# An attention core regrouped: one 512-column context product for four heads, in place of one 65-column product for each head

## The reference, cut to what matters

```python
# L0 attention, 1024 tokens of 256 features; H, NOPE, ROPE, V_DIM, KV_RANK = 16, 128, 64, 128, 64
q = (hidden_states @ q_proj_w.T).reshape(b, s, H, Q_DIM).transpose(0, 2, 1, 3)
compressed = hidden_states @ kv_a_proj_w.T
k_pass_lat = compressed[..., :KV_RANK]
k_rot = compressed[..., KV_RANK:]
kv = _rmsnorm(k_pass_lat, kv_a_ln_w) @ kv_b_proj_w.T        # per head: k_pass (128), v (128)
scores = jnp.einsum('bhqd,bhkd->bhqk', q, k) * scaling      # causal
probs = jax.nn.softmax(scores.astype(jnp.float32), axis=-1).astype(q.dtype)
out = jnp.einsum('bhqk,bhkd->bhqd', probs, v)
return out.transpose(0, 2, 1, 3).reshape(b, s, H * V_DIM) @ o_proj_w.T
```

## Time and profile before

| | before |
|---|---|
| median of 3 runs | 997.33 us |
| runs | 988.61, 997.33, 999.35 us |
| span of the profiled execution, first to last instruction | 985.5 us |
| attention, first transposes of tile 1 to the last tile's residual | 84.2 to 472.3 us of the span |
| PE busy in that stretch | 374.84 of 388.10 us |
| PEld, DVE, ACT, POOL busy there | 329.48, 224.91, 185.27, 133.04 us |

### The profile page before, as it was taken

How to read it: one execution, slowest core, us unless ns; L and a number is a source line. 1 busy time by engine, 2 the same in 40 slices (tenths; PEclk the granted TensorE clock), 3 DMA queues, 4 the chain that set the end, 5 groups by cost and what they waited for, 6 DMA issues and landing times.

```text
span 985.5 us, 17100 instructions
## 1 busy us (share of the span) xinstructions
PE 850.1 (86%) x5125; PEld 700.9 (71%) x5126; DVE 452.2 (46%) x1231; ACT 322.4 (33%) x768; POOL 261.2 (27%) x432
## 2 busy tenths in 40 slices
PE   5999998999999999998279993476888799999964
PEld 4778886788999888887179992466866555556653
DVE  4123664647475665664334442466755122222244
ACT  1233554654554444443024341121232022222210
POOL 2003535242414132134300003777306000000241
PEclk9997999999999999998589997698989999999988
DMA  6339401010001000001569994556352111111111
GB/s 172 83 93 415 149 1 43 7 39 12 32 2 43 2 26 18 2 27 60 204 209 352 355 358 131 177 171 212 125 171 80 33 43 43 43 43 32 49 59 38
DMA packets 83856, 102.20 MB, mean 104 GB/s; under 512 B 16096, under 2 KB 74464, under 8 KB 82528
## 3 DMA queue, kind: packets, MB, share of 16 engines
q1 hardware_dynamic: 64112, 69.20, 21.7%
q0 software_dynamic: 7680, 20.98, 6.5%
q10 hardware_dynamic: 12016, 11.41, 3.4%
HBM read 67.22 MB, written 34.34 MB: 103 GB/s over the span
## 4 chain that ended last, share of the span: by engine, by line
PE 33%; POOL 7%; issue 5%; DVE 3%; DMA 2%; ACT 0%; POOLq 0%; SPq 0%; DVEq 0%; ACTq 0%
PE scores L1634 9%; POOL area L569 6%; PE scores L1484 5%; PE acc_ps L1654 4%; PE probsT_ps L1598 3%; PE scores L1495 2%; PE scores L1287 2%; PE probsT_ps L1473 1%; PE scores L1288 1%; PE scores L1289 1%; DMA area<-xe_d 1%; PE probsT_ps L1644 1%; POOL rstd L517 1%; POOL xe_d L525 1%; PE misc_ps L1619 1%
## 5 line engine op out<-in xcount | busy, mean ns | idle before, releaser
L1384 PE MATMUL misc_ps<-area 128*128 128x65 f32 x1152 | 152.5, 278 | 4.7 <-DVE ctx_n L903 1.6
L1384 PEld LDWEIGHTS misc_ps<-area 128*128 128x128 f32 x1152 | 146.5, 196 | 11.0 <-ACT area L649 2.5
L887 DVE TENSOR_REDUCE neg_max<-scores 128x1 f32<-128x128 f32 (+7 forms) x128 | 96.8, 756 | 67.6 <-PE scores L1358 64.8
L511 POOL TENSOR_TENSOR q_lo<-area,q_hi 128x128 fp32r<-128x128 f32 x128 | 59.1, 461 | 179.7 <-ACT q_hi L668 171.4
L649 ACT COPY area<-probsT_ps 128x512 f32<-128x512 f32 (+3 forms) x128 | 64.9, 507 | 120.0 <-PE probsT_ps L1368 115.4
L643 ACT ACTIVATE area<-scores,neg_max 128x128 f32<-128x128 f32 (+7 forms) x128 | 95.7, 747 | 0.0
L1368 PE MATMUL probsT_ps<-ident,area 128*128 128x128 f32 x576 | 91.0, 281 | 2.1 <-ACT ctxT L653 1.8
L1634 PE MATMUL scores<-area 128*128 x184 | 86.7, 615 | 4.0 <-issue 2.9
L1287 PE MATMUL scores<-kT_hi,q_hi 128*128 128x512 f32 (+3 forms) x192 | 77.3, 402 | 6.3 <-POOL q_lo L511 4.8
L1368 PEld LDWEIGHTS probsT_ps<-ident,area 128*128 128x128 f32 x576 | 69.1, 149 | 7.6 <-ACT ctxT L653 6.9
L569 POOL DMA_INDIRECT area<-ye_d,fetch_now x64 | 63.9, 999 | 23.5 <-issue 18.5
(11 more groups left out here) (217 smaller groups left out, 1496.4 us busy)
## 6 DMA issues: line engine op xcount, KB each, us to landing
area<-gate_up SPq DMA_DIRECT2D x32, 384.0 KB, 6.9
xe_d<-area SPq DMA_DIRECT2D x8, 1024.0 KB, 10.3
area<-w SPq DMA_DIRECT2D x8, 1024.0 KB
area<-xe_d SPq DMA_DIRECT2D x32, 256.0 KB, 7.0
ye_d<-area ACTq DMA_DIRECT2D x32, 256.0 KB, 5.9
area<-down SPq DMA_DIRECT2D x32, 192.0 KB, 7.1
area<-w SPq DMA_DIRECT2D x8, 512.0 KB, 7.9
area<-xd_d SPq DMA_DIRECT2D x23, 128.0 KB, 2.2
```

The source lines that it names most:

```text
L887: dve.tensor_reduce(neg_max[:, u:u + 1], banks[u][:, 0:(qt + 1) * P], AX.X, ALU.max, negate=True).then_inc(max_ready, 1)
L1384: last = pe.matmul(ctx_ps, probsT[:, u, k * P:(k + 1) * P], latent[:, k, :], start=k == 0, stop=k == qt)
```

## The change

Heads are taken in groups of four. A slot is one head's turn: group G, head i of four, `n = 4G + i`. In slot n the scores of head n + 2 are made, the steps of group G - 1 and the output of one head of group G - 2 (`output(4(G - 2) + i)`), so that three groups are under way at once. All loops over pairs are gone; every instruction of the attention stands in the program once.

- Transposes of one block of all four heads go to one bank (`transpose_probs(G, k)`), ScalarE copies the whole bank (`copy_hi`), and `context(G, k)` holds the 128x64 block of `latent` as weights and moves 512 columns of transposed probabilities. There are 144 such products, one for each group and block, in place of 576.
- The context comes out transposed (64 partitions by 4 x 128 columns); ScalarE copies it once for a group (`copy_ctx`), and the 64 transposes of the context go.
- The output is made for each head, with 64 partitions: 128 products of 256 columns in place of 64. They aren't accumulated in PSUM: VectorE multiplies each with the inverse row sum and adds it to x1 (`add_head`), and the next one waits for that (`out_read`), since they share one bank. Row sums come from the exponential's own accumulator.
- The read-outs of the router move to the second half of the outputs' bank (`acc`). `pe_slot` waits for `out_read` before each of the three steps, and for the step's read-out before the next output.
- GpSimd makes both halves of the query, for two heads at once and three pairs ahead; ScalarE's rounding goes. Sends are issued one in every second slot.
- Rows of probabilities of ten heads are kept, in a part of the memory for expert weights, so the first loads of expert weights wait for the last transposes. The zero rows become half as long. The `wvo` products have both halves of the partitions filled and are copied as 512 columns.

```diff
...
+QUAD = 4
+SETS = HEADS // QUAD
+GROUPS = TILES * SETS
+ROWS_KEPT = 10
...
+        wv_h = cutA3(2, 2, RANK)
...
+        wvo = cutA3(HEADS * HID)
...
+        latent = wq_h.rearrange("p a b -> p (a b)").rearrange("p (t r) -> p t r", t=TILES)
...
+        pT_sb = cutA3(2, BANK)
...
-        x1T_ps = pT[1][:, 0:HID]
...
+        out_ps = acc[:, 0:HID]
+        x1T_ps = acc[:, HID:2 * HID]
...
+        def steps_at(G, place):
+
+
+            if not 0 <= G < GROUPS:
+                return []
+            n = tile_of(G) + 1
+            return [k for k in range(n + 1) if k * 8 // (n + 1) == place]
+
...
+        def head_slots(body):
+
+            for G in range(GROUPS + 2):
+                for i in range(QUAD):
+                    body(G, i, QUAD * G + i)
...
+            sp.wait_ge(pT_ps, blocks_to(GROUPS))
...
+            def split_q(m):
+
+                qt, h = divmod(2 * m, HEADS)
+                two = qT[:, h * T:(h + 2) * T].rearrange("p (h t) -> p h t", h=2)[:, :, qt * P:(qt + 1) * P]
+                if m >= 3:
+                    pool.wait_ge(scores_ready, 2 * (m - 3) + 2)
+                pool.tensor_copy(q_his[m % 3], two).then_inc(q_half, 1)
+                pool.wait_ge(q_half, m + 1)
...
+            def copy_hi(b):
+                act.wait_ge(pT_ps, b + 1)
+                if b >= 2:
+                    act.wait_ge(ctx_step, b - 1)
+                act.copy(pT_sb[:, b % 2, :], pT[b % 2][:]).then_inc(hi_done, 1)
+
+            def copy_ctx(G):
+                act.wait_ge(ctx_step, blocks_to(G + 1))
+                if G >= 2:
+                    act.wait_ge(out_ready, QUAD * (G - 1))
+                act.copy(ctxT[0:RANK, G % 2, :], ctx_ps[0:RANK, :]).then_inc(ctx_copied, 1)
...
+            def act_slot(G, i, n):
+                for place in (2 * i, 2 * i + 1):
+                    for k in steps_at(G - 1, place):
+                        if k <= tile_of(G - 1):
+                            copy_hi(blocks_to(G - 1) + k)
+                if i == QUAD - 1 and 0 <= G - 1 < GROUPS:
+                    copy_ctx(G - 1)
+                if n + 2 < TILES * HEADS:
+                    exp_probs(n + 2)
+                if G >= SETS + 2 and G % SETS == 2 and i == 2:
+                    copy_x1T(tile_of(G) - 1)
...
+            def add_head(n):
+
+                t, h = divmod(n, HEADS)
+                s, k = stat_of(n)
+                dve.wait_ge(out_ready, n + 1)
+                if h == 0:
+                    dve.wait_ge(ld_x, 16)
+                    dve.wait_ge(rinv_done, n // QUAD + 1)
+                else:
+                    dve.wait_ge(out_read, n)
+                dve.scalar_tensor_tensor(x1[:, t, :], out_ps, rinv[:, s, k:k + 1], x1[:, t, :] if h else x_in[:, t, :],
+                                         ALU.mult, ALU.add).then_inc(out_read, 1)
...
+            def dve_slot(G, i, n):
+                if n + 2 < TILES * HEADS:
+                    row_max(n + 2)
+                if i == 1 and 0 <= G - 1 < GROUPS:
+                    invert(G - 1)
+                t = tile_of(G) - 1
+                if t >= 0 and (G % SETS, i) == (2, 3):
+                    read_logits(t)
+                if t >= 0 and (G % SETS, i) == (3, 1):
+                    read_place(t)
+                if 0 <= G - 2 < GROUPS:
+                    add_head(QUAD * (G - 2) + i)
+                if t < 0:
...
+            def transpose_probs(G, k):
+                b = blocks_to(G) + k
+                pe.wait_ge(probs_ready, QUAD * (G + 1))
+                if b >= 2:
+                    pe.wait_ge(hi_done, b - 1)
+                for i in range(QUAD):
+                    last = pe.transpose(pT[b % 2][:, i * P:(i + 1) * P], row_of(QUAD * G + i)[:, k * P:(k + 1) * P],
+                                        ident[:])
+                last.then_inc(pT_ps, 1)
+
+            def context(G, k):
+                b = blocks_to(G) + k
+                pe.wait_ge(hi_done, b + 1)
+                if k == 0:
+                    if G:
+                        pe.wait_ge(ctx_copied, G)
+                    else:
+                        pe.wait_ge(lat_split, 1)
+                pe.matmul(ctx_ps[0:RANK, :], latent[:, k, :], pT_sb[:, b % 2, :], start=k == 0,
+                          stop=k == tile_of(G)).then_inc(ctx_step, 1)
+
+            def output(n):
+                G, i = divmod(n, QUAD)
+                pe.wait_ge(ctx_copied, G + 1)
+                if n:
+                    pe.wait_ge(out_read, n)
+                h = n % HEADS
+                pe.matmul(out_ps, ctxT[0:RANK, G % 2, i * P:(i + 1) * P], wvo[0:RANK, h * HID:(h + 1) * HID],
+                          start=True, stop=True).then_inc(out_ready, 1)
...
+            def steps(G, place):
+                for k in steps_at(G, place):
+                    if k <= tile_of(G):
+                        transpose_probs(G, k)
+                    if k:
+                        context(G, k - 1)
+
+            def pe_slot(G, i, n):
+                t = tile_of(G) - 1
+                g = G % SETS
+                if t >= 0 and (g, i) in ((2, 2), (2, 3), (3, 1)):
+                    pe.wait_ge(out_read, QUAD * (G - 2) + i)
+                    if (g, i) == (2, 2):
+                        transpose_x1(t)
+                    elif (g, i) == (2, 3):
+                        route(t)
...
+                        count_places(t)
+                steps(G - 1, 2 * i)
+                if n + 2 < TILES * HEADS:
+                    scores(n + 2)
+                steps(G - 1, 2 * i + 1)
+                if 0 <= G - 2 < GROUPS:
+                    if t >= 0 and (g, i) == (2, 2):
+                        pe.wait_ge(x1T_done, t + 1)
+                    if t >= 0 and (g, i) == (2, 3):
+                        pe.wait_ge(logits_read, t + 1)
+                    if t >= 0 and (g, i) == (3, 1):
+                        pe.wait_ge(place_read, t + 1)
+                    output(QUAD * (G - 2) + i)
+            head_slots(pe_slot)
             transpose_x1(TILES - 1)
```

393 lines of the change are left out of this document (105 added, 288 removed).

## The result

The changed kernel takes **1127.56 us** (median of 4 runs, 1123.37 to 1130.6), the kernel before beside it 996.48 (988.61 to 999.35): a ratio of **1.131** with a 95% interval of 1.125 to 1.137. It is slower, as forecast, but by 131 us where 53 were forecast. The profiled execution spans 1128.9 us at a mean granted clock of 0.899 (before 985.5 and 0.932).

The account below looks back on a forecast made before the run. TensorE's work was taken as the bound from tile 5 on. Terms -4 + 23 + 14 + 10 + 7 + 5 + 4 + 4.6 + 6 - 16 gave +53 us, 1050 us; own range 1030 to 1062, 8-in-10 range 1008 to 1082.

Parts of the forecast that it names:

- Context products ... 0.88 each: TensorE's attention: 144 full-precision products of 512 columns at 0.88 us, 126.7 us against 131.0 before, a term of -4.
- Outputs at 0.48: TensorE's attention: 128 output products of 256 columns at 0.48 us, 61.4 us against 38.1 before, +23.
- The clock falls at the router's slots: Rival: in tiles 2 to 8 idle waits at router steps lower TensorE's clock, +12 to +24 us, 1068; 22%.
- (a): Before each of 21 router steps TensorE waits for VectorE's add of the output just issued: 0.67 us each, 14 us.
- I let all 16 go: Tiles 2 to 4: TensorE's 16 us of pauses, from chains through GpSimd and ScalarE, all vanish, -16.
- 4 + 4.6 + 6: Small terms: `choose` and `assign` holding adds 4 us, tile 8's shared transposes 4.6, attention's start and end 6.
- (b): The output in slot (2,2) waits for ScalarE's copy of x1T behind an exponential, tiles 2 to 8: 10 us.
- (c): The output in slot (2,3) waits for the logits, read behind VectorE's row maximum, tiles 2 to 8: 7 us.
- (d): The output in slot (3,1) waits for the places, read behind a maximum and small reciprocal: 5 us.
- Two of the small terms: Tile 8's wait for a block's copy, 4.6 us, and `choose` and `assign` holding the next add, 4 us.
- The rival of cheap narrow operands: Rival: 64-column context and 64-row output products each cost half, context 0.44 us, giving 956 us; 5%.

Follow-up runs that it names:

- the version with the late router: Changed kernel with both narrow products made full, logits, places and x1T read at their slots' heads, router products behind the scores: 989.98 us, ratio 1.021.
- narrow pair: Kernel before with each pair's output as two 64-row products instead of one over 128 rows: 1025.08 us, ratio 1.049; twin with two full products 1.026.
- the two versions with early read-outs and narrow shapes: Changed kernel with logits, places and x1T read at their slots' heads: 1074.14 us, ratio 1.099; also with router products behind the scores: 1082.07 us, 1.087.
- their counterparts with full shapes: Those two versions with context and output products both made 128 by 128: 1002.82 us, ratio 1.032, and 989.98 us, ratio 1.021.
- the early read-outs: Changed kernel with ScalarE's x1T copy and VectorE's readings of logits and places moved to their slots' heads: 1074.14 us, ratio 1.099.
- the repeat: Changed kernel run once more without an edit, against the kernel before: ratio 1.129 (1.115 to 1.143).

## Why the prediction was wrong

The direction was right and most waits were. The time lies outside the range, by 46 us.

**"Context products ... 0.88 each": the step that failed first.** The row it rests on the earlier trace rows is a stream of full 128-by-128 products. With 64 weight columns between neighbours of 128 the product takes 1.00 us, and the transposes ahead of it 0.53 instead of 0.46. 144 x (0.12 + 0.07) = 27 us, and the term -4 becomes +23. With full shapes the same product takes 0.86 (in the version with the late router 192.73 - 191.87), so the price was right for the shape that it was read from.

**"Outputs at 0.48".** They take 0.63: 128 x 0.15 = 19 us more. The forecast asked whether few rows are cheaper and found them not to be; that they could be dearer was not among its bounds. The 96-row product was the nearest row, but its records' length was read, not its distance to neighbours of another shape. What the Trainium skill says on the page quoted there (TensorE: Matmul & The Clock Gate, "Why this matters for your kernels"), that a single small product takes as long as a full one, held inside a narrow pair (0.216 us a pass in either shape) and not for one narrow product among full ones, 0.63 against 0.44. Another page of the Trainium skill (TensorEngine Tiling (Array Packing), "Key Properties") has the rule that was missed: changing the tiling mode, and not just the tile, drains the engine. The traces agree: the next shape's weights are loaded only when the product before is over, and a way into a narrow pair and out takes 0.22 us.

Together shape costs 46 us in distances. The experiments say 66 for shape; the other 20 are put down to the clock by difference. The windows bear out most of it: the two versions with early read-outs and narrow shapes have 40 us at 1.2 GHz in the attention's first 40 us, their counterparts with full shapes 8 and 6, and half of the difference is 16 to 17.

**"The clock falls at the router's slots": the right suspect in the wrong place.** The rival was priced at 12 to 24 us, by falls after waits. Such falls are there and cost 14 us (the early read-outs remove them). But the larger part is at the attention's start, where no router stands: by the windows shown (0.50, 0.50, 0.55) 2 x (0.5 x 20 + 0.5 x 20 + 0.45 x 26) = 63 us at 1.2 GHz with TensorE busy throughout. The forecast gave no term to a clock that stays low without pauses. How long it lasts is partly luck of the execution: in the three other traces of both shapes narrow, with the same order up to there, the window from 124 to 150 us has 0.81 (the repeat), 1.00 and 1.00. What decides that moment was not found.

**The waits: right.** (a) was priced at 0.67 us a step, 14 us; the router's product now starts 1.27 us after an output instead of 0.63, 21 x 0.64 = 13.4, and the late router got back 11 to 13. The row maximum and the exponential of five blocks last 823 and 796 ns as before, with 194 ns for the accumulator behind, as allowed. (b), (c) and (d) were priced at 10, 7 and 5; TensorE's waits are 8.0, 5.3 and 2.7 us. In tile 3 the copy was to cost 1.81 us and costs 200.20 - 198.35 - 0.16 = 1.69. Removing them paid about 30 us instead of 16, and the clock is what is left to explain the rest.

**"I let all 16 go": hardly any went.** With full shapes and short waits tiles 2 to 4 take 32.8 + 39.8 + 48.4 = 121.0 us against 113.9 before, at full clock. The new work explains 3 (16 heads by 0.13 for the output less 0.021 T for transposes and context). Work of the next tile explains about 6: counted in the traces, the new windows hold 6 transposes, two context products and some 7700 columns of scores more than the old ones, priced here at the forecast's prices. By this estimate about 2 of the 16 went. The count also shows that 16 was too many: the old windows held next tiles' work too, 4 us of it. The old waits did go. In tiles 2 to 4 TensorE waited 4.2 us for GpSimd's half of the query and 1.6 for the normalised context, and in the version with the late router for neither, but 6.5 us for adds, read-outs and a block's copy. The sum of that version doesn't decide it: without shapes the remaining terms are -7 (context at 0.86) + 17 (outputs at 0.43) + 4 + 4.6 + 6 and 3.5 us of waits left, +28, or +12 with the 16 taken off; measured are +21 (14 to 28).

**What the forecast's sum becomes.** 53, + 46 for shapes, + 25 for the start at 1.2 GHz (half of 63 less the 2 x 0.34 x 20 = 14 of before), + 12 for falls later (14 less the 1.7 of before), + 15 for the slower code behind the attention, less 6 for smaller (b) to (d): 145, against a span longer by 143.4. The closeness is partly luck, for that sum still counts all 16 of the pauses as gone. Two of the small terms were too high: in tile 8 TensorE waits 1.1 us for a block's copy where 4.6 were priced, and `choose` and `assign` show as one wait of 1.3 us for an add where 4 were priced. With these and with 2 of the 16 it is 145 + 14 - 6 = 153, so some 10 us of the account stay open. The median lies 1.3 below the span here and lay 11.8 above it in the forecast. Each run's time is 1.7 us above its own span, so those differences are between executions; the ratio of 1.131 is the sounder measure.

**The rival of cheap narrow operands** fell as far as it could: not 0.44 us for a context product, and not 0.88, but 1.00.

## What to carry to other kernels

Look at the shape that a product has in the array (weight rows by columns, "128*64" in a trace) next to that of its neighbours before pricing it: a narrow product amid full ones cost its streaming time plus a switch on each side, here 0.07 to 0.15 us a switch, and filling the array with copies or zeros made the whole changed kernel 6% faster. Price a product by the distance between starts in a stretch with the same neighbours; where no such stretch exists, the bound must reach above the full product's price too. And look at the granted clock behind waits of TensorE that come close together: here 16.0 us of them came with some 14 us lost to the clock.

## What was not expected of the hardware

- TensorE at 20.00 of 20 us busy with both narrow shapes in the stream was granted 0.50, while the same stream with full shapes, at 17.25 of 20, was granted 0.95. Busy time alone did not bring the clock back.
- Two narrow products in a row cost one switch in and one out, 0.22 us; the step between them is a full product's.
- Waits of up to 1.9 us at three places of a tile came with about as much again lost to the clock (16.0 us of waits, 14 of clock); with them gone, the clock stayed at 1.00 from 124 to 560 us, although 21 waits for adds, 13.3 us in all, were still there.
